# Two attention blocks of a transformer kernel: batch parts stored before any is loaded, gathers moved to the front, row sums on VectorE

## What is computed

```python
x = x + _L0_xattn_ref(_layernorm(x), ctx_1024, ctx_1024, mask, Wq, Wk, Wv, Wout, b_out, 1)   # causal
x = x + _L0_ffn_ref(_layernorm(x), ...)        # 16 experts of width 512, top 2
x = x + _L1_xattn_ref(_layernorm(x), ctx_1024, ctx_1024, ctx_1024, Wq, bq, ..., Wo, bo)       # all keys
x = x + _L1_ffn_ref(_layernorm(x), ...)        # 7 experts of width 1024, top 2, and a shared one

# an attention
q, k, v = split_heads(h @ Wq), split_heads(ctx @ Wk), split_heads(ctx @ Wv)
scores = q @ k.T / 4 (+ masks, causal triangle in the first)
out = (softmax(scores) @ v) @ Wo + bo
```

## Time and profile before

| | |
|---|---|
| median of 3 runs | 1475.82 us (1469.08 to 1478.23) |
| the profiled execution | 1471.67 us, its span 1470.0 us |
| PE busy | 1165.3 us, 79% of the span |
| DVE, ACT, POOL busy | 719.9, 585.0 and 402.2 us |
| mean granted clock of PE | 0.888 of full speed |
| DMA | 182.26 MB in 94170 packets, 124 GB/s over the span |

### The profile page before, as it was taken

How to read it: one execution, slowest core, us unless ns; L and a number is a source line. 1 busy time by engine, 2 the same in 40 slices (tenths; PEclk the granted TensorE clock), 3 DMA queues, 4 the chain that set the end, 5 groups by cost and what they waited for, 6 DMA issues and landing times. The chain is left out here.

```text
span 1470.0 us, 26772 instructions
## 1 busy us (share of the span) xinstructions
PE 1165.3 (79%) x8532; PEld 1009.6 (69%) x8532; DVE 719.9 (49%) x1623; ACT 585.0 (40%) x1184; POOL 402.2 (27%) x601
## 2 busy tenths in 40 slices
PE   4689986765359999626565875699999999999997
PEld 3466764554358888513333544699999999999997
DVE  6545544444212222267444675555555555555556
ACT  1355653411112322115454672244444444444432
POOL 5267662013501111263556301260000000000062
PEclk8699998857779999857888897599999999999999
DMA  6645766004479999543344332112233223223132
GB/s 164 112 114 139 164 145 191 1 1 127 144 298 327 329 326 332 188 110 67 76 94 85 54 55 93 58 63 73 65 107 96 80 90 95 86 85 96 52 87 87
DMA packets 94170, 182.26 MB, mean 124 GB/s; under 512 B 15843, under 2 KB 64413, under 8 KB 87824
## 3 DMA queue, kind: packets, MB, share of 16 engines
q1 hardware_dynamic: 81776, 141.40, 35.6%
q0 software_dynamic: 12320, 39.94, 7.8%
HBM read 134.29 MB, written 47.72 MB: 124 GB/s over the span
## 5 line engine op out<-in xcount | busy, mean ns | idle before, releaser
L1972 PE MATMUL e_ps<-xT_e,wp_e 128*128 128x384 f32 (+1 forms) x1344 | 245.0, 331 | 4.8 <-DVE wp_e L1846 4.8
L699 DVE TENSOR_REDUCE att_ps<-att_ps 128x2 f32<-128x512 f32 (+1 forms) x224 | 154.9, 697 | 185.5 <-PE att_ps L963 103.1
L1972 PEld LDWEIGHTS e_ps<-xT_e,wp_e 128*128 128x128 f32 x1344 | 221.6, 188 | 6.2 <-issue 4.9
L961 PE MATMUL att_ps<-ks,qs 96*128 96x256 bf16 (+1 forms) x512 | 109.5, 282 | 88.0 <-DMA qs<-parts 46.6
L886 ACT ACTIVATE probs<-att_ps 128x384 f32<-128x384 f32 (+1 forms) x256 | 130.5, 544 | 48.2 <-PE att_ps L993 37.3
L1902 DVE TENSOR_TENSOR hid_e<-act_a_e,e_ps 128x256 f32<-128x256 f32 (+2 forms) x176 | 87.0, 494 | 115.4 <-ACT act_a_e L1804 106.8
L1804 ACT ACTIVATE act_a_e<-e_ps 128x256 f32<-128x256 f32 (+2 forms) x176 | 77.8, 442 | 159.9 <-PE e_ps L1972 159.2
L1989 PE MATMUL e_ps<-wp_e,hidp_e 128*128 128x256 f32 (+1 forms) x1008 | 138.3, 281 | 3.0 <-DVE xres L1862 1.2
L1904 DVE TENSOR_TENSOR hidp_e<-hid_e,hidp_e 128x256 fp32r<-128x256 f32 (+2 forms) x176 | 87.7, 498 | 95.5 <-ACT hidp_e L1808 95.5
L1808 ACT ACTIVATE hidp_e<-hid_e 128x256 fp32r<-128x256 f32 (+2 forms) x176 | 83.8, 476 | 127.0 <-DVE hid_e L1902 125.3
L1989 PEld LDWEIGHTS e_ps<-wp_e,hidp_e 128*128 128x128 f32 (+1 forms) x1008 | 130.5, 183 | 5.0 <-issue 4.1
(11 more groups left out here) (216 smaller groups left out, 1980.9 us busy)
## 6 DMA issues: line engine op xcount, KB each, us to landing
w_e<-in_W SPq DMA_DIRECT2D x48, 1024.0 KB, 7.6
w_e<-in_W SPq DMA_DIRECT2D x57, 384.0 KB, 3.0
ks<-parts SPq DMA_DIRECT2D x96, 128.0 KB, 5.0
qs<-parts SPq DMA_DIRECT2D x96, 128.0 KB, 4.1
parts<-cut SPq DMA_DIRECT2D x24, 384.0 KB, 5.6
rows<-zeros POOLq DMA_DIRECT2D x8, 768.0 KB, 4.9
x_e<-rows SPq DMA_DIRECT2D x48, 128.0 KB, 6.4
done<-y_e POOLq DMA_DIRECT2D x48, 128.0 KB, 6.3
```

Of the source, the lines that this page charges most:

```text
L699: dve.tensor_reduce(tops_at(at[3])[:, qt, x0:x0 + heads], src, AX.X, ALU.max).then_inc(reduced, 1)
L961: last = pe.matmul(out, qs[0:KS, j, hd, qt * P:(qt + 1) * P], ks[0:KS, j, hd, 0:keys(qt)], start=True, stop=not causal)
L1972: last = pe.matmul(ps[:, bank + u % 2, 0:n], weights(lot, c, pw)[:, (b * DC + d) * P:(b * DC + d + 1) * P], xT[:, px, d, t0:t0 + n], start ...
```

## The change

Constants: the block of its own goes; POOL makes the constants at the start of the first attention block, with semaphores for their users, and the other engines start there at once.

Layout on the host: `x` and the masks are laid out by partition, so that their loads are contiguous.

SP's queue: see the diff and the rows below. For batches from 2 on, both parts are stored, then both stacks loaded; the load of the context of f stands at the head of turn f and no longer one turn ahead. `x` of batches 1 and 2 comes in the second load, the rest (batches 3 to 7) and the masks of batches 2 to 7 after the stacks of batches 0 and 1. In layer 1 the loads of `ks` for batches 0 and 1 wait until the gathers of that batch have landed.

POOL: in layer 1 all 32 gathers come ahead of the batches (12, the ones and values of batch 0, then 20), the signal `rows_here` is given once, after all of them have landed and the bias of batches 0 and 1 is joined. The sums go to DVE. In layer 0 the roots go to DVE, where batches 3 to 7 share one; `join_bias` stands ahead of split q.

DVE: `combine` is now one instruction for each tile and expert, four a batch, in group 0; `root` is 13 instructions with fused forms; moments of batches 3 to 7 of layer 0 all stand in groups 1 and 2 of batch 0. It sets half of the mask rows of `ks` in batch 0 and closes the mask of batch 0.

ACT: `norm_rows` of batch f moves from slots 12 and 13 of batch f - 3 to slots 0 and 1 of batch f - 2.

```diff
-            for f in range(B):
+            for f in range(FEED):
+                for i, w in enumerate(KINDS):
+                    store(f, i, w)
+                    sp.wait_ge(parts_stored[f], 16 * (i + 1))
+                    load_stack(sp, stacks[w], f, parts_dram, w, f, stacks_loaded[f])
+            if x is not None:
+                load_x(2)
+            if causal:
+                load_flags(1)
+            for f in range(FEED, B):
                 j = f % 2
-                if ctxT is not None and 2 <= f + 1 < B:
-                    load_context(f + 1)
-                if f >= FEED:
-                    sp.wait_ge(scoredT, (f + 1) * H)
-                    if 1 not in KINDS:
-                        load_stack(sp, ks, j, parts_dram, 1, f, stacks_loaded[j])
+                if ctxT is not None:
+                    load_context(f)
                 for i, w in enumerate(KINDS):
-                    sp.wait_ge(parts_ready[w], f + 1)
-                    store_parts(sp, parts_dram, w, f, parts[:, j, i], parts_stored[j])
-                    sp.wait_ge(parts_stored[j], 16 * (len(KINDS) * (f // 2) + i + 1))
+                    store(f, i, w)
+                sp.wait_ge(scoredT, (f + 1) * H)
+                if 1 not in KINDS:
+                    load_stack(sp, ks, j, parts_dram, 1, f, stacks_loaded[j])
+                sp.wait_ge(parts_stored[j], 16 * len(KINDS) * (f // 2 + 1))
+                for w in KINDS:
                     load_stack(sp, stacks[w], j, parts_dram, w, f, stacks_loaded[j])
...
             for n in range(B):
                 f = n + FEED
-                if ye is not None and normed_ahead(n):
-                    add_rows(n + NORM)
                 if n + 1 < B:
                     values(n + 1)
-                if fed(n) and 1 in KINDS:
-                    split(pool, f, 1)
-                if normed_ahead(n):
-                    root(pool, n + NORM)
+                if fed(n):
+                    if 1 in KINDS:
+                        split(pool, f, 1)
+                    join_bias(f)
+                if normed_ahead(n) and ye is not None:
+                    pool.wait_ge(spread_ready, n + 1)
+                    root(pool, n + NORM, 1, False).then_inc(root_ready, 1)
                 if fed(n):
                     split(pool, f, 0)
                     if causal:
-                        close(f)
-                    join_bias(f)
-                if ye is not None and n + GATHER < B:
-                    gather(n + GATHER)
+                        close(pool, f)
                 clear_rows(n)
...
+            def combine(f, t, c):
+                xt = xres_tile(f, t)
+                dve.scalar_tensor_tensor(out=xt, in0=back[:, bass.ds(f, 1), t, c, :].rearrange("p a d -> p (a d)"),
+                                         scalar=m["gate"][:, c, bass.ds(f * TPB + t, 1)], in1=xt, op0=ALU.mult, op1=ALU.add)
...
-                        if g == 1 and u == 0 and normed_ahead(n):
+                        if g == 0 and u == 0 and gathered:
+                            dve.wait_ge(rows_here, 1)
                             dve.wait_ge(root_ready, f - 1)
-                            if ye is not None:
-                                dve.wait_ge(rows_here, n + 1)
                         if more:
                             reduce(after(at), u)
-                        if g == 1 and normed_ahead(n) and u < TPB:
-                            moments(f, jf, u)
+                        if g == 0 and gathered:
+                            t, c = u % TPB, u // TPB
+                            if u == TPB:
+                                dve.drain()
+                            combine(f, t, c)
```

More of the change, by code:

```diff
@@ L101, in alloc @@
     return m
[L104 to L125, removed]
 def rstd_steps_vector(dve, m, var_ready, root_ready):
@@ new lines, in stats_at, with root, of @@
+        def stats_at(f, ring, t):
+            return NT + ring[0] * TPB + t if ring else f * TPB + t
+        def root(eng, f, n, fused):
+            def of(ap, lo=f * TPB):
+                return ap[:, lo:lo + n * TPB]
+            y, nh, b, a, off = of(rstd), of(spread), of(bits), of(near), of(offset)
+            at = stats_at(f, (f % 2,) if ye is not None and f >= NORM else None, 0)
+            mean, var = of(mean_var[:, :, 0], at), of(mean_var[:, :, 1], at)
+            eng.tensor_scalar(nh, var, LN_EPS, None, ALU.add)
+            eng.drain()
+            eng.tensor_copy(b, nh.bitcast(I32))
+            eng.tensor_scalar(nh, nh, -0.5, None, ALU.mult)
@@ L653, in _ @@
             join_bias(1)
+            if ye is not None:
+                for loaded in back_loaded:
+                    pool.wait_ge(loaded, 16 * 2 * TPB)
+                pool.sem_inc(rows_here, 1)
             if fill:
@@ L743, in aggregate, with set_keys @@
                 dve.tensor_copy(m["mv"][:, bass.ds(n * TPB, TPB), :], mv[:])
+            def set_keys(j):
+                for g in range(NG):
+                    last = dve.tensor_copy(ks[KS:KT, j, g * G:(g + 1) * G, :], m["minus"][KS:KT])
+                last.then_inc(keys_set, 1)
             def batch(n, j, r, first, last):
-                f, jf = n + NORM, 1 - j
+                f = n + NORM
+                gathered = ye is not None and normed_ahead(n)
                 for g in range(NG):
@@ L767, in batch @@
                         normalize(prior(at))
[L768 to L769 removed]
+                    if g == 0 and first:
+                        set_keys(1)
+                        if ye is None:
+                            dve.wait_ge(x_loaded[2], 16)
+                    if g == 1 and gathered:
+                        dve.drain()
+                        averages(f, (1 - j,)).then_inc(spread_ready, 1)
+                    if g == 2 and first and ye is None:
+                        dve.drain()
+                        for i in range(NORM, B):
+                            averages(i)
@@ new lines, in _ @@
+            prepare(0, 1)
+            if 1 in KINDS:
+                split(dve, 0, 1)
+                prepare(1, NORM - 1)
+                split(dve, 0, 0)
+            else:
+                prepare(1, 1)
+                split(dve, 0, 0)
+                prepare(NORM - 1, 1)
+            if constants:
+                dve.wait_ge(minus_ready, 1)
+            set_keys(0)
+            if causal:
+                dve.wait_ge(later_ready, 1)
+                close(dve, 0)
+            if 1 in KINDS:
+                split(dve, 1, 1)
@@ L2041, in lay_out @@
     c = np.ascontiguousarray
-    mask = i["mask_BxSxS2_bf0"]
+    masks = np.stack([i["mask_BxSxS2_bf0"], i["mask_BxSxS2_bf0"].transpose(0, 2, 1)])
     def by_channel(w):
```

235 lines of the change are left out of this document (131 added, 104 removed).

## The result

The changed kernel takes 1483.12 us (median of 20 runs, 1472.92 to 1488.64), the one before 1472.76 us on the same chip (20 runs, 1459.48 to 1482.74). The ratio is 1.0064 with a 95% interval of 1.0044 to 1.0084: slower by some 10 us. The interval leaves out "no change", but 10 us is less than the 1% that the prediction called a change. The forecast was 1478 and "within 1%". One of the four runs of the first experiment took 1962.46 us at a mean granted clock of 0.549, where the other three had 0.90; its median of 1405.89 counts that run, and is 1405.22 without it.

The account below looks back on a forecast made before the run. PE's waits in attention, for q stacks in layer 0 and DVE in layer 1, were the bound. Layer 0 +46.2 and layer 1 -43.6 gave +2.6 on 1471.67, 1474.3, or 1478 as median; range 1464 to 1492, with rivals A and B 1450 to 1506.

Parts of the forecast that it names:

- The bound before: PE waits in attention: layer 0 for q stacks, 25.9 us; layer 1 for DVE, held by POOL's sum, 41.4 us.
- The context becomes late: Layer 0, batches 1 to 5: context behind twelve stack loads lands at 15.0 us; PE stands 12.6 us at slot 0.
- Rival A: Layer 0: clearing transfers meet the twelve loads, context lands near 19.5 instead of 15.0, +22, 1500 us; chance 0.27.
- Steady state: Layer 0, batches 1 to 5: 119.5 us of work plus 5 x 15.0 gives 194.5 against 144.9, +49.6.
- Rival B: Layer 0: the context overtakes the stack loads and lands at 11.0, taking 20 off, 1458 us; chance 0.15.
- Start of layer 0: Earlier start lost waiting for batch 2's context, -0.5; DVE's added work in batch 0, +3; together +2.6 us.
- Batch 7: Layer 0: its 12.31 us wait is halved, as clearing transfers still meet the stack loads: -6, bounds 0 and -12.
- Layer 1: Attention: four waits go, -40.0; earlier start, -3.6; DVE's products set against a faster PE clock; -43.6 us, bounds -33 and -52.
- Rival C: All waits in layer 0 go, as the change's order suggests, besides layer 1's gain: about 1391 us; chance 0.05.
- Rival D: Layer 1: gathers take 2.3 us each instead of 1.30, so the signal comes 20 us later, 1498 us; chance 0.05.

Follow-up runs that it names:

- the first experiment: Changed kernel with the context of batch f + 1 sent at the head of turn f, that of batch 2 between the first two batches' stacks: 1405.89 us.
- the early signal: The kernel of the first experiment with x and masks loaded early and layer 1's gathered rows signalled batch by batch, ahead of the biases: 1391.07 us.

## Why the prediction was right, and where it was not

The sum came out at +2.6 and the traces give +12.3, the medians of the runs +10.4; the forecast of "within 1%" holds, with a gain in layer 1 eaten by a loss in layer 0, as it said. The 1478 had 4.2 us in it for the distance of the median from the profiled execution; with 20 runs that distance is 1.1. Point by point:

- **The bound before** was read rightly: the two groups of waits were what the change took away, and both are gone.
- **The context becomes late**, the central step: right in its place (slot 0 of batches 0 to 5, released by `cst`), in its size (12.6 us predicted, 12.4 measured) and in the landing (15.0 predicted, 15.0 measured). But the landing was right by two errors. Twelve loads alone give 13.6, so "1.3 + 13.2 + 0.5" was 1.4 too long; and the clearing, which I had put 6 us ahead of the transposed scores, goes out 0.2 us behind the first stack load (2.0 in the first of the five turns) and adds 1.4. Rival A had its mechanism, not its price.
- **Steady state** +49.6 predicted, +52.4 measured. The missing term is the clock: the remaining work was taken as 119.5 us, as in the kernel before, and took 197.2 - 62.1 - 11.8 = 123.3; PE is busy 134.9 us in it, 131.0 before. The prediction priced the clock's gain from removed waits in layer 1 and forgot its loss from new ones here.
- **Rival B**, a context that overtakes, is false: twelve loads ahead of it delay it from 4.1 to 13.6 us.
- **Start of layer 0** +2.6 predicted, -3.9 measured. The first score came at 31.3 instead of 35 and the keys of batch 2 at 53.97 instead of 59. Most of these 5 us is the second stack, sent at 40.35 and not at 44; from there to the keys it took 13.6 us where "1.3 + 6.6" and "2.3 MB at some 340 GB/s" made 15. From the keys to the end of the transposed scores are 23.8 us, 21.9 before, so 1.9 where the prediction had "+3" for DVE's work in batch 0.
- **Batch 7** -6 predicted, -8.5 measured in its wait.
- **Layer 1** -43.6 predicted, -29.9 measured, the largest error. Its start was right: first score 36.6 us behind the first gather predicted, 37.3 measured; the signal 48.6 predicted, 49.7 measured, although what released it was the landing of the last rows and not POOL, which was through with the two biases 2.7 us earlier. What failed is the step "at some 0.35 us each that is 1.4 us [...] I let it stand against the faster PE clock": the duration was taken from DVE's four products with the gates at the start, and each costs 0.615 us in the loop. The clock gave nothing to set against it: 0.82 over the whole attention in both traces, and the same 1344 products keep PE busy for 170.9 us before and 177.1 after. The pace was 25.9 us where 23.2 was forecast; taking the products out gives 22.9, of which some 2.0 us are theirs.
- **Rival C**, about 1391, was dismissed because of the order of SP's queue, and that order was the main obstacle: with the context ahead the kernel takes 1405.9. The 1391.1 of the early signal meets rival C's number with two edits that the change doesn't have.
- **Rival D** did not happen: the gathers went out every 1.25 us in the trace, as the 1.30 before. Its price was too low: 32 gathers of 1.0 us more each would have put the signal 32 us later, not 20.

So the errors by the books were -6.5 (start), +2.8 (steady state), -1.8 (batch 7 and what follows), +13.7 (layer 1) and +1.4 behind it, 9.6 together, for the 9.7 between +2.6 and +12.3. The two large ones have opposite signs, so the sum is nearer than its terms: in part that is luck.

## To carry to other kernels

When transfers are put in a new order to shorten one chain, write down for every transfer of that queue what now stands ahead of it and when its user asks; a transfer that is asked for first belongs first, even behind the same wait. Price a new hole in PE as longer than itself; here each of 12.4 us cost another 1.8 in slower products behind it, 8.9/5. If work is moved to relieve a waiting engine, ask first whether an earlier start of its inputs removes the wait with the work left where it is.

## What I had not expected

- A context of 256 KB with nothing ahead of it lands in 3.2 to 3.9 us (medians; 4.9 at most) although 1.5 MB of stack loads follow it at once, and 1.5 MB of clearing from POOL's queue 0.24 us later.
- Clearing from POOL's queue slows SP's issuing: the six `ks` loads take 4.4 to 5.9 us to send when it goes out within 0.3 us of them, and without it 2.7 to 3.6, once 4.2. The clearing isn't all of it: six `qs` loads took 4.2 to 4.6 us in one turn of each of the three kernels without it. Why SP is held wasn't tried.
- The granted clock of PE in layer 1 differs between traces of kernels whose layer 1 has the same program, 0.87 to 0.90 or 0.96 over 120 us of it, and the block takes 244 to 246 us or 239. Why wasn't tried.
- DVE's product-and-add of 128x256 in float32 costs 0.47 us at the start of the block (four in 1.89) and 0.615 in the mean of the loop; why wasn't tried. DVE's plain products with the gates took 0.33 before (1.31 for four), a different instruction, so its price was no price for the new one.
